# Attention block on Trainium2: group statistics moved to ScalarE and GpSimd, residual additions moved on GpSimd's queue

## The reference

```python
def _gn(v, G=32, eps=1e-5):
    g = v.reshape(B_, G, C_ // G, H_, W_)
    m = jnp.mean(g, axis=(2, 3, 4), keepdims=True)
    s = jnp.var(g, axis=(2, 3, 4), keepdims=True)
    return ((g - m) / jnp.sqrt(s + eps)).reshape(v.shape)

q, k, v4 = (conv1x1_bn(x, ...) for each)       # 256, 256 and 1024 channels
vl = depthwise 3x3 of v4, scaled and shifted
attn = einsum('bhid,bhjd->bhij', q, k) * SCALE + ab[:, BIAS_IDXS]
attn = softmax(einsum('bhij,gh->bgij', attn, th1w) + th1b)
attn = einsum('bhij,gh->bgij', attn, th2w) + th2b
o = relu(einsum('bhij,bhjd->bhid', attn, v) + vl)
x = x + conv1x1_bn(o, pw, pb, p_s, p_t)        # with x normalised by _gn on the way in only
```

## Time and profile before

| | us | |
|---|---|---|
| median of three runs | 4653.12 | |
| the profiled execution | 4652.12 | its span is 4650.3 |
| TensorE matmul | 4567.8 busy | 98% |
| VectorE | 4405.2 busy | 95% |
| ScalarE | 3370.8 busy | 72% |
| GpSimd | 1128.9 busy | 24% |
| granted TensorE clock | 0.998 of full speed | |

### The profile page before, as it was taken

One profiled execution on the slowest core, in us unless ns is written; L12 is line 12 of the kernel. 1 busy time (PEld: TensorE's weight loads), 2 busy tenths in 40 slices (PEclk: granted clock), 3 DMA queues, 4 the chain that ended last, 5 costly groups with the idle time before them and its releaser, 6 DMA issues.

```text
span 4650.3 us, 108573 instructions
## 1 busy us (share of the span) xinstructions
PE 4567.8 (98%) x33794; PEld 4530.7 (97%) x33794; DVE 4405.2 (95%) x10833; ACT 3370.8 (72%) x7941; POOL 1128.9 (24%) x1093
## 2 busy tenths in 40 slices
PE   6999999999999999999999999999999999999999
PEld 6999999999999999999999999999999999999999
DVE  8999999999999999999999999999999999999998
ACT  5777777777777777777777777777777777777776
POOL 2222122122221222222212222122122221222212
PEclk9999999999999999999999999999999999999999
DMA  2223223222232232222322223223222232222322
GB/s 90 80 70 88 63 79 90 68 79 75 67 94 63 79 84 68 84 63 78 94 64 79 79 65 93 63 79 84 72 80 68 74 94 63 79 79 67 90 63 74
DMA packets 210781, 356.02 MB, mean 77 GB/s; under 512 B 15986, under 2 KB 132738, under 8 KB 210692
## 3 DMA queue, kind: packets, MB, share of 16 engines
q1 hardware_dynamic: 210756, 355.71, 27.7%
HBM read 199.67 MB, written 155.98 MB: 76 GB/s over the span
## 4 chain that ended last, share of the span: by engine, by line
PE 71%; issue 15%; DVE 13%; DVEq 0%; POOL 0%; DMA 0%; ACT 0%; POOLq 0%; SPq 0%
PE psA L288 38%; PE psA L423 11%; PE psM L288 10%; PE psL L288 10%; DVE psC L686 8%; DVE shared L686 2%; DVE probs L743 1%; DVE shared L785 1%; DVE nmax L743 0%; PE psA L306 0%; DVEq L680 0%; DVE rinv L764 0%; PE psA L301 0%; DVE q_lo L710 0%; DMA qa<-by_key 0%
## 5 line engine op out<-in xcount | busy, mean ns | idle before, releaser
L686 DVE SCALAR_TENSOR_TENSOR psC<-vpad,par,psC 128x406 f32<-128x406 f32 x3072 | 1795.4, 633 | 0.0
L561 ACT ACTIVATE probs<-probs,nmax 112x196 f32<-112x196 f32 x1792 | 799.5, 449 | 177.0 <-DVE nmax L743 168.7
L288 PE MATMUL psA<-x_hi,w_lo 128*128 128x392 f32 x2304 | 795.5, 345 | 8.5 <-DVE x_lo L667 8.5
L288 PE MATMUL psA<-x_lo,w_hi 128*128 128x392 f32 x2304 | 789.0, 342 | 0.0
L288 PE MATMUL psA<-x_hi,w_hi 128*128 128x392 f32 x2304 | 788.0, 342 | 0.0
L423 PE MATMUL psA<-qa,shared 105*128 105x196 f32 x4096 | 710.3, 332 | 50.4 <-DVE shared L785 49.3
L423 PEld LDWEIGHTS psA<-qa,shared 105*128 105x128 f32 x4096 | 677.8, 191 | 69.6 <-DVE shared L785 68.3
L710 DVE SCALAR_TENSOR_TENSOR q_lo<-qk,th,q_hi 128x392 fp32r<-128x392 f32 x1024 | 663.8, 677 | 0.0
L458 ACT ACTIVATE o_hi<-shared 128x392 fp32r<-128x392 f32 x512 | 264.8, 529 | 468.0 <-DVE shared L785 468.0
L466 ACT ACTIVATE q_hi<-qk,th 128x392 fp32r<-128x392 f32 x1024 | 595.6, 620 | 2.1
L840 POOL TENSOR_TENSOR k_lo<-qk,k_hi 128x392 fp32r<-128x392 f32 x128 | 168.0, 1312 | 1700.5 <-ACT k_hi L470 1700.5
(11 more groups left out here) (81 smaller groups left out, 10391.3 us busy)
## 6 DMA issues: line engine op xcount, KB each, us to landing
by_key<-probs SPq DMA_DIRECT2D x512, 224.0 KB, 3.8
qa<-by_key SPq DMA_DIRECT2D x128, 448.0 KB, 4.3
qk<-by_key SPq DMA_DIRECT2D x128, 448.0 KB, 6.9
xs<-in_x SPq DMA_DIRECT2D x64, 588.0 KB, 4.4
shared<-in_x SPq DMA_DIRECT2D x64, 588.0 KB, 3.8
out<-shared SPq DMA_DIRECT2D x63, 588.0 KB, 3.1
qa<-in_wqkv SPq DMA_DIRECT2D x3, 768.0 KB, 6.8
stage_wp<-in_wp SPq DMA_DIRECT2D x1, 1536.0 KB, 10.8
```

Source lines behind the costliest of these rows:

```text
L288: last = nc.tensor.matmul(dst, w, r, start=(begin and n == 0), stop=(end and n == 2))
L561: nc.scalar.activation(row, row, ACT.Exp, bias=nmax[:, img, b:b + 1], scale=-1.0, accum_out=rowsum[:, img, b:b + 1]).then_inc(s_exp, 1)
L686: nc.vector.scalar_tensor_tensor(a if tap == 7 else sums, src, taps[:, c, TAPS[tap]:TAPS[tap] + 1], a if tap == 0 else sums, MUL, ADD).the ...
```

## The change

The group statistics of all pairs but the first are taken by ScalarE: a copy and a square over each image with the accumulator giving sum and sum of squares. They are written into `proj` as unused output, between the centre taps and the first of the projections' evictions. One matmul with a 128 x 128 matrix `same` both sums over a group's partitions and gives the result back to each of them, so `g_sum`, `g_bc` and `group_broadcast` go. ScalarE copies the sums out of PSUM after the sixth row of exponentials. GpSimd computes variance and reciprocal deviation in four instructions on 128 partitions and normalises by (x - mean) x rstd. On VectorE the statistics and the five small instructions between the scores go; for the first pair it keeps them (`first_stats`, `first_moments`). On GpSimd all three residual blocks now stand behind the mixing weights, and the fill of `probs` with ones stands behind the first pair's variance.

```diff
             def group_sums(p):
-                pe.wait_ge(s_stat, p + 1)
-                nc.tensor.matmul(psA[0:GROUPS, 1, 0:4], g_sum[:, :], mv[:, :, :]...
+                nc.tensor.matmul(psA[:, 1, 0:4], same[:, :], mv[:, :, :]...
-            def group_broadcast(p):
-                pe.wait_ge(s_gval, p + 1)
-                nc.tensor.matmul(psA[:, 1, 8:12], g_bc[:, :], g_val[:, :, :]...
...
                     if n == 2 and not last:
                         if not first:
                             pe.wait_ge(s_pout, 3 * (t - 1) + 2)
+                        pe.wait_ge(s_stat, 4 * (t + 1))
                         group_sums(t + 1)
-                    elif n == 10 and not last:
-                        group_broadcast(t + 1)
...
                 if not last:
-                    pe.wait_ge(s_ab, t + 2)
+                    pe.wait_ge(s_gs, t + 2)
...
+            def stats(p):                                   # ScalarE
+                act.wait_ge(s_x, 16 * (p + 1))
+                unused = proj[:, :, :].rearrange("p k n -> p (k n)")
+                for i in range(2):
+                    src = xs[:, i, :, :].rearrange("p k n -> p (k n)")
+                    for n, (func, scale) in enumerate(((ACT.Copy, SUM_SCALE), (ACT.Square, SQUARE_SCALE))):
+                        if i:
+                            act.wait_ge(s_stat, 4 * (p - 1) + n + 1)
+                        nc.scalar.activation(unused[:, n * RUN:(n + 1) * RUN], src, func,
+                                             scale=scale, accum_out=mv[:, i, n:n + 1]).then_inc(s_stat, 1)
+            def group_moments(p):
+                act.wait_ge(s_gsum_mm, p + 1)
+                nc.scalar.copy(gs[:, :, :]..., psA[:, 1, 0:4]).then_inc(s_gs, 1)
...
                 conv_centre(t, 2)
                 conv_centre(t, 3)
+                if not last:
+                    stats(t + 1)
+                    act.wait_ge(s_stat, 4 * (t + 1))
                 if not first:
                     projected(t, 0)
                     projected(t, 1)
...
+                    if n == 5 and not last:                 # in the rows of exponentials
+                        group_moments(t + 1)
...
-                if not last:                                # VectorE, head of the step
-                    stats(t + 1)
...
-                    if 3 <= n < 6 and not last:             # VectorE, between the scores
-                        group_variance(t + 1, n - 3)
-                    elif n == 8 and not last:
-                        group_values(t + 1)
-                    elif n == 12 and not last:
-                        channel_values(t + 1)
...
+            def reciprocal_deviation(p):                    # GpSimd
+                pool.wait_ge(s_gs, p + 1)
+                nc.gpsimd.tensor_tensor(g_msq[:, :], gs[:, :, 0], gs[:, :, 0], MUL).then_inc(s_gmsq, 1)
+                nc.gpsimd.tensor_tensor(g_var[:, :], gs[:, :, 1], eps[:, :], ADD).then_inc(s_gvar, 1)
+                wait_alone(pool, s_gmsq, p + 1)
+                wait_alone(pool, s_gvar, p + 1)
+                nc.gpsimd.tensor_tensor(g_sub[:, :], g_var[:, :], g_msq[:, :], SUB).then_inc(s_gsub, 1)
+                wait_alone(pool, s_gsub, p + 1)
+                nc.gpsimd.tensor_tensor(rstd[:, :], g_sub[:, :], mhalf[:, :], ALU.pow).then_inc(s_rstd, 1)
...
-                if not first:                               # GpSimd, in the step, behind k_lo
-                    pool.wait_ge(s_res, 16 * t)
-                    residual(t, 0)
-                    residual(t, 1)
                 if not last:
-                    rstd(t + 1)
+                    reciprocal_deviation(t + 1)
                     normalise(t + 1)
                 mixing_weights(t, first, 0)
                 mixing_weights(t, first, 1)
...
                 if not first:
-                    residual(t, 2)
+                    pool.wait_ge(s_res, 16 * t)
+                    for m in range(CT):
+                        residual(t, m)
```

More of the change, by code:

```diff
@@ L37 @@
 EPS = 1e-5
+RUN = CT * PIX
+SUM_SCALE, SQUARE_SCALE = 2.0 ** -10, 2.0 ** -5
 GAP = 2 * RES * QT * HP - VT // 2 * ACC - 4 * DH
@@ L68, in build @@
         kron2 = sb("kron2", [HP, NH, RES])
-        g_sum = sb("g_sum", [P, GROUPS])
-        g_bc = sb("g_bc", [GROUPS, P])
+        same = sb("same", [P, P])
         small = sb("small", [HP, 2 * NH + RES + 1])
-        mhalf = sb("mhalf", [GROUPS, 2])
+        mhalf = sb("mhalf", [P, 2])
+        eps = sb("eps", [P, 2])
         xs = sb("xs", [P, 2, CT, PIX])
@@ L223, in _ @@
             load_x(0)
-            sp.dma_start(g_sum[:, :], A["g_sum"]).then_inc(s_gconst, 16)
-            sp.dma_start(g_bc[:, :], A["g_bc"]).then_inc(s_gconst, 16)
+            sp.dma_start(same[:, :], A["same"]).then_inc(s_gconst, 16)
             w_rows = A["wqkv"].rearrange("(p k) m -> k p m", p=P)
@@ L299, in group_sums @@
             def group_sums(p):
-                pe.wait_ge(s_stat, p + 1)
-                nc.tensor.matmul(psA[0:GROUPS, 1, 0:4], g_sum[:, :], mv[:, :, :].rearrange("p i s -> p (i s)"),
+                nc.tensor.matmul(psA[:, 1, 0:4], same[:, :], mv[:, :, :].rearrange("p i s -> p (i s)"),
                                  start=True, stop=True).then_inc(s_gsum_mm, 1)
-            def group_broadcast(p):
-                pe.wait_ge(s_gval, p + 1)
-                nc.tensor.matmul(psA[:, 1, 8:12], g_bc[:, :], g_val[:, :, :].rearrange("p i s -> p (i s)"),
-                                 start=True, stop=True).then_inc(s_gbc_mm, 1)
             def project(t, m, whole):
@@ L323, in project @@
                 last.then_inc(s_proj_mm, 1)
[L325 removed]
+            pe.wait_ge(s_gconst, 16)
+            pe.wait_ge(s_mv, 3)
             group_sums(0)
[L327 removed]
             def bias_table():
@@ L612, in constants, with first_stats @@
                 nc.vector.tensor_tensor(l_t, l_t, l_b, ADD).then_inc(s_ready, 1)
-            def stats(p):
-                dve.wait_ge(s_x, 16 * (p + 1))
+            def first_stats():
+                dve.wait_ge(s_x, 16)
                 for n in range(4):
                     i, half = divmod(n, 2)
-                    run = CT * PIX // 2
                     src = xs[:, i, :, :].rearrange("p k n -> p (k n)")
-                    nc.vector.bn_stats(bst[:, i, half, :], src[:, half * run:(half + 1) * run]).then_inc(s_bst, 1)
-                wait_alone(dve, s_bst, 4 * (p + 1))
+                    nc.vector.bn_stats(bst[:, i, half, :],
+                                       src[:, half * (RUN // 2):(half + 1) * (RUN // 2)]).then_inc(s_bst, 1)
+                wait_alone(dve, s_bst, 4)
@@ L654, in weights_low @@
                                         SUB).then_inc(s_wlo, 1)
-            stats(0)
-            for n in range(3):
-                group_variance(0, n)
-            group_values(0)
+            first_stats()
+            first_moments()
+            dve.wait_ge(s_rstd, 1)
+            for i in range(2):
+                nc.vector.tensor_scalar(xs[:, i, :, :], xs[:, i, :, :], gs[:, i, 0:1], rstd[:, i:i + 1], SUB, MUL).then_inc(s_xn, 1)
             weights_low(0)
-            channel_values(0)
-            for i in range(2):
-                dve.wait_ge(s_ab, 1)
-                nc.vector.tensor_scalar(xs[:, i, :, :], xs[:, i, :, :], ab[:, i, 0:1], ab[:, i, 1:2], MUL, ADD).then_inc(s_xn, 1)
             weights_low(1)
@@ L829, in mixing_weights @@
                                             MUL).then_inc(s_mixw, 1)
-            rstd(0)
+            pool.wait_ge(s_eps, 1)
+            reciprocal_deviation(0)
+            nc.gpsimd.memset(probs[:, :, :, :], 1.0).then_inc(s_ones, 1)
             pool.wait_ge(s_whi, CT)
@@ L897 @@
         "ones": np.ones((1, TURNED), np.float32),
-        "g_sum": member * np.float32(CT / GC),
-        "g_bc": member.T,
+        "same": member @ member.T * np.float32(1 / (GC * PIX * SUM_SCALE)),
         "small": np.concatenate([np.repeat(a["th1w"].T, RES, axis=0), np.repeat(a["th2w"].T, RES, axis=0),
```

60 lines of the change are left out of this document (22 added, 38 removed).

## The result

The changed kernel took 4587.15 us, median of six runs (4579.72, 4580.5, 4585.53, 4588.78, 4589.47, 4630.72), against 4652.72 (4651.62 to 4653.68) for the kernel before. The ratio is 0.987, interval 0.983 to 0.991. The forecast of 4650.5 was wrong, and the time lies under its range of 4597 to 4690; rival 1, at 4600, is the nearest of the cases. The spread of 51 us is itself new: the kernel before spreads over 2 us.

The account below looks back on a forecast made before the run. TensorE was taken to bound each pair until the score of n = 11, then VectorE to its first addition; +0.16, 20.63 and +0.80 gave -0.04 us a pair, -2.6 us with start and ends, 4650.5 us, range 4597 to 4690.

Parts of the forecast that it names:

- rival 1: GpSimd's residual additions miss VectorE's taps of the last channel pair: -0.84 us a pair, 4600 us; chance 0.15.
- the stretch from n = 10: Score of block n = 10 to VectorE's first addition: 20.63 us instead of 21.63, as in the last pair.
- The third addition: GpSimd's third residual addition meets VectorE's first tap of the last channel pair: 0.80 us a pair, bounds 0 and 1.03.
- If VectorE wins the tie: VectorE's tap starts before GpSimd's third addition, which then comes between the two taps: some 0.78 us lost.
- The sums matmul: TensorE's group sums matmul, after n = 2, loads 128 columns instead of 32: +0.16 us a pair, bounds 0 and 0.31.
- The start: Fill of probs moves behind GpSimd's small instructions, delaying its part of w_lo and the first matmul: +1.0 us, bounds 0 and 2.
- Start and first pair together: Start +1.0 us; in the first pair wp_lo comes earlier and releases the tap waiting behind it: -1.9 us.
- Statistics: Four ScalarE activations before the projections' evictions: 3.2 us a pair, at most 5.6, priced at 0.
- cover: ScalarE's idle time before the second projection and the slack until TensorE's next sums matmul: 6.3 us for the statistics.
- the copy of the sums: ScalarE's copy among the exponentials, bounded by 0 and half a cast: priced at 0.
- GpSimd's small instructions and normalisation: On GpSimd after the sums are copied: 3.4 us, at most 4 x 0.9 + 3.24, so GpSimd waits for the reciprocal.
- Rival 3: VectorE's first tap of the third channel pair starves behind image 0's mixing weights: 2.2 us a pair, 4789 us; chance 0.12.

Follow-up runs that it names:

- e4: The kernel before with both group matmuls and the small instructions between them padded to 128 x 128: 4625.66 us, ratio 0.994.
- e5: e3 with four statistics and two joining instructions put back on VectorE in every pair, results unused: 4584.46 us, ratio 0.985.
- e2: The changed kernel with the first of the three residual additions between the mixing weights of the two images: 4628.99 us, ratio 0.995.
- e7: The changed kernel with one unused 0.15 us GpSimd instruction ahead of the three residual additions: 4628.71 us, ratio 0.995.
- e9: e3 with GpSimd's fill of probs ahead of the first pair's variance again: 4575.82 us, ratio 0.983.
- e10: e9 with ScalarE's four statistics activations issued a second time in every pair, results unused: 4582.4 us, ratio 0.985.
- e6: The kernel before with only the residual additions moved, all three behind the mixing weights: 4795.97 us, ratio 1.030.
- e3: The changed kernel with the residual additions where they stood before, two behind k_lo, one behind the mixing weights: 4578.14 us, ratio 0.984.
- e1: The changed kernel run again without any edit, for the spread of its times: 4629.1 us, ratio 0.995.
- e8: The changed kernel with four unused 0.15 us GpSimd instructions ahead of the three residual additions: 4669.77 us, ratio 1.004.

## Why the prediction was wrong

**What bounds the kernel, and the stretch from n = 10: right.** The last pair of the kernel before was the right row to go by. The middle pair now takes 2078.45 - 2057.83 = 20.62 us against a forecast of 20.63 from the earlier trace rows, without collision. Little of this came from the instructions taken off VectorE, though. The time from the score of n = 10 to the second reciprocal fell from 6.79 us to 6.30, because TensorE's broadcast no longer delays the score of n = 11 (1.66 us after that of n = 10 before, 1.40 with the cheaper broadcast of e4, 1.19 now), and the last taps fell from 1.70 to 1.20, because no addition lies under them. A microsecond of VectorE counts only in this stretch: 2.0 us of statistics at the head are worth 0.10 (e5), 0.82 behind n = 10 are worth 0.81 (e2).

**The third addition: the step that failed.** The prediction's arrival times are right to 0.01 us: additions at reciprocal + 3.58, + 4.56 and + 5.54, tap at + 5.55. It then said that the pair costs some 0.8 us whoever is first, for "If VectorE wins the tie, the addition comes between the two taps". The case of the earlier trace rows, from which it took that, is an addition that comes in the course of an instruction of VectorE; e7 makes the same case here and gives the same loss. In the tie proper there is a third outcome that no row of before showed: VectorE goes ahead with both taps, and the addition takes 1.07 us longer, for which nobody waits (its row in the middle pair: 4.05 against 2.98). 0.80 of the 1.18 us a pair by which the forecast was off is this term. Where GpSimd wins, the price was well sized: 0.81 measured, 0.80 forecast. What decides the tie is open: the lost pairs were 2 of 63 in one run, 47 in another and, by the time, nearly all in others of the same program, and the third addition's start against the tap's is the same in both kinds to 0.03 us. Rival 1, with its window "before + 4.7 or after + 6.6", came near the measured time by another mechanism, which is luck: its sign, both taps at 0.6 us, was there, but the additions do not miss the taps, they lose to them.

**The sums matmul: wrong in sign.** Priced at + 0.16, it is worth 0.33 - 0.22 = -0.11 us, and e4 shows it without the rest of the change. The prediction read the 0.15 on the chain as its whole price and left out the 0.18 by which the matmuls behind it ran longer. That makes 0.27 of the 1.18. The remaining 0.10 is the faster pace of the projections' matmuls, which e5 gives back and the prediction did not have.

So 0.80 + 0.27 + 0.10 = 1.17 us a pair, against 1.22 - 0.04 = 1.18. Over 62 pairs that is 73 us, less 3.6 at the start (next paragraph): the 4649.5 of the sum becomes 4580, and the profiled run took 4580.5.

**The start: + 1.0 forecast, + 4.0 measured** (23.11 - 19.09 at the first projection). The fill ends where it was to end, at 14.43. But on VectorE the normalisation of the first pair, 1.08 us before, takes 8.82 beside fill and w_lo: its first instruction can't pass the fill, its second ends 0.3 us behind w_lo. The prediction went by GpSimd's queue and not by who shares its port. e9 shows it by moving the fill: 1.08 there, and 2.27 for the small scaling now under it, while two VectorE instructions with two SBUF inputs (L644 and L646) ran under the same fill in 0.16 us each. The Trainium skill (SBUF — State Buffer, section "Who interferes with whom") says that a VectorE instruction in a mode that uses both ports contends with GpSimd, and one with two SBUF inputs only with a GpSimd instruction that reads SBUF. The traces agree, since a fill only writes. This is 2.4 of the 4.0 us; the other 1.6 fit the new place of VectorE's first part of `w_lo` (e9), which the prediction did not price. In the first pair the last taps took 8.11 us behind wp_lo and x_lo, where the prediction had taken 1.9 off. Start and first pair together are + 2.7, forecast -0.9.

**ScalarE and GpSimd: right.** Statistics 2.9 us (forecast 3.2), second projection still waiting for TensorE, cover confirmed by e10; the copy of the sums 0.14 us; GpSimd ready before the reciprocal (idle 2.07). GpSimd's small instructions and normalisation end at 2056.72, 6.4 us after the copy and not 3.4, for the normalisation in its new form takes 2.33 us for each image, not 0.96. The bound of 4 x 0.9 + 3.24 = 6.8 covered the sum of both only just, and the half of it that was taken, 3.4, did not.

**Rival 3** did not come in the changed kernel (tap at 2059.58 with 0.65 us) but for the first pair, where it cost 0.76 us. e2 and e6 have its mechanism: 0.82 us where the tap got in after one instruction of GpSimd, 2.45 where it didn't.

## What to carry to other kernels

A tie of two engines for the port they share has no one price: move one side clear of it (e3 has 0.95 us) instead of pricing it, since the same program gave 4580 and 4630 us. Price a small matmul by the chain with the matmuls behind it, and pad it to the full array if its shape is narrow. Before moving a long GpSimd instruction, a fill too, list every VectorE instruction that could meet it, not only what is queued behind it. And before a gain is put down to the instructions that were taken away, see which wait in the bounding stretch became shorter.

## What the runs showed of the hardware

- VectorE and GpSimd at the port they share, two taps of 0.55 us against one addition of 1.03: recorded starts within 0.03 us of each other, VectorE loses 0 or 0.81 us (first profile and e1); addition 0.14 us into the first tap, 0.76 us, in every pair (e7).
- A waiting VectorE instruction can be passed over by GpSimd's next one that follows without a gap: 1.40 us lost in all 63 pairs of e8, 2.45 us in 34 of 62 middle pairs of e6, while in the other 28 VectorE got in after the first addition.
- After TensorE had waited 2.6 us, its granted clock read 0.50 and 48 matmuls took 9.91 us or more instead of 8.23, in 29 of 34 cases (e6).
- A VectorE TENSOR_SCALAR of 0.17 us took 2.27 us under GpSimd's fill, while two TENSOR_TENSOR with two SBUF inputs took 0.16 us each under it (e9).
- Matmuls of 128 x 32 and 32 x 128 with four columns cost TensorE 0.33 and 0.50 us in a stream of 128 x 112 ones; 128 x 128 costs 0.22.
- A two-operation GpSimd instruction over 588 elements took 2.33 us in the form (x - mean) x rstd and 0.96 in the form before. The cause is open.
